# A four-layer graph network on one core: register range checks dropped, the edge network's sums moved to the front of VectorE's round, the first attention's one-hot moved to ScalarE

## The chip, the cores and the metric

The program runs on one core of a Trainium2 chip (trn2). The metric is the device time of one execution in microseconds (us); the number that counts is the median of several executions. A core has five engines that run side by side, each through its own instruction stream in order: TensorE (PE, with its weight loads listed as PEld), VectorE (DVE), ScalarE (ACT), GpSimd (POOL) and SyncE (SP). They wait for each other through semaphores. Each stream is driven by a sequencer (DVEq, ACTq, SPq in the rows), which also executes register arithmetic and which has to finish that before it can pass the next instruction to its engine.

## The reference

Four message-passing layers over 3125 nodes and 100000 edges, each on `h = relu(layernorm(x))`, each added to `x`. Edges are sorted by target `dst`. Cut to what matters:

```python
# layer 0, edge network (MLP)
h1  = relu([h[src], h[dst], edge_attr] @ We1 + be1)
em  = relu(h1 @ We2 + be2)
h2  = relu([h[dst], em] @ Wn1 + bn1)
x  += h + segment_sum(relu(h2 @ Wn2 + bn2), dst)
# layer 1, first attention: 4 heads, softmax over the edges of a target with its maximum taken off
e   = elu(s_src[src] + s_tgt[dst], 0.2);  ex = exp(e - segment_max(e, dst)[dst])
x  += segment_sum(ex / segment_sum(ex, dst)[dst] * xp[src], dst)
# layer 2, second attention: 8 heads, leaky relu, softmax without the maximum
# layer 3, relations: 16 weight matrices, chosen by the edge's type, summed by src
```

## The kernel before

The edges are cut into 208 blocks of 512 (`N_BLOCKS`, `BLOCK`); a block is two halves of 256 edges or four tiles of 128. All edges of a half have targets in one bin of 128 nodes. Four stages, one for each layer, run one after the other with a short node phase between them (normalisation, the node matrices and a table of rows in HBM). In each stage every block goes through the same steps:

- GpSimd fetches the source rows of a block from the table by four indirect DMAs, one for each tile (`gather`, L1032). ScalarE writes the indices that they use (`lay`, L1023); in the last stage VectorE does.
- VectorE compares the block's target numbers with 1..128. This gives the one-hot `hot` (edges by nodes), the left side of the matmul that sums a half's messages into its bin (`mm_sum`), and `hot_t`, the transposed one, which spreads target rows over edges.
- TensorE does the matmuls. `mm_sum` leaves two sums in a PSUM bank.
- VectorE adds the two sums to the accumulator `acc` at the bins of the halves (`add_sum`, L1335). Which bin that is stands in a table of numbers in SBUF, `bin_d`; `halves_of` (L997) loads eight of its numbers into registers at every fourth block. SyncE loads the halves' start addresses and, in the first attention, ScalarE loads bins, by the same helper.

`values_load_multi_w_load_instructions` with `min_val` and `max_val` emits one TENSOR_LOAD and, for each of the eight numbers, register arithmetic and an assertion that stops the program if the number is outside its range.

The order on each engine is written out by hand: `pipeline` and `unrolled` take a list of `(lag, stage)`. In round `k` an engine runs each stage of its list, in the list's order, for block `k - lag`. Nothing reorders it.

**Edge network (`edge_mlp`).** VectorE's round before is: `localize`, `make_hot_t`, `bring_dst` of block k, `nm_relu` of k-4, `make_hot` of k-2, `add_sum` of k-5, and then one small piece of a sort that the last layer needs. TensorE's round is `turn` (k-1), `mm_h2` (k-3), `mm_h1` (k-2), `mm_sum` (k-4), `mm_em` (k-2), `mm_nm` (k-3), `mm_q` (k-2). There is a single PSUM bank for the sums, so `mm_sum` of a block waits until `add_sum` of the block before has been done; it also waits for `nm_relu` of its own block.

**First attention (`softmax_sum`).** Groups of eight blocks share the steps that find the maxima: TensorE brings scores into lanes (`lanes`), ScalarE copies them out (`to_lanes`, L1575), VectorE scans (`tops`), TensorE turns back (`back`, L1632), VectorE subtracts (L1697), ScalarE takes the exponential (`weight`, L1581). In each block VectorE scales the rows (`message`, L1704) and makes `hot` (`make_hot`, L1709) from a copy of 1..128 in PSUM, TensorE sums (`mm_sum`, L1641), and ScalarE copies the sums out of one of two PSUM banks (`keep_sum`, L1590); `mm_sum` of block k waits for `keep_sum` of block k-2. The gather of a block waits for `mm_sum` of the block 16 before.

The two attentions' ScalarE streams and all streams of GpSimd and SyncE contain a hardware loop of 16 blocks a turn; VectorE's in the edge network and the second attention are written out in full.

## Time and profile before

| | us |
|---|---|
| median of three runs | 5009.35 (5000.32 to 5012.24) |
| the profiled execution's own time | 5033.62 |
| its span | 5031.8 |

Busy time over the span: PE 3496.0 (69%), PEld 2811.4 (56%), DVE 2828.2 (56%), ACT 1003.1 (20%), POOL 3291.4 (65%). No engine is busy all the time, and an average over the span says little, since the four stages have different limits. By stage the profile goes: ordering and first tables up to about 107 us; edge network up to 1343; node phase; first attention 1400 to 2665; node phase; second attention 2723 to 3805; node phase; relations 3945 to 5032.

In a timeline row the columns are start, duration, engine, line, operation with what it writes and reads, how many instructions are merged, and in brackets the idle time before it with what ended it. "issue" there means that the engine waited for nothing that the profile shows: often its own sequencer.

### The profile page before, as it was taken

The page shows a single profiled execution, that of the slowest core. Times are in us where ns is not written, and L with a number is a line of the kernel's source. Part 1 is how long each engine was busy: PE and PEld are TensorE (multiplying, and loading weights), DVE is VectorE, ACT ScalarE, POOL GpSimd, SP SyncE. Part 2 cuts the span into 40 slices and gives each one's busy share as a digit, 9 for nine tenths or more (in the row PEclk, how much of TensorE's full clock was granted, in tenths as well). Part 3 has the DMA queues.
Part 4 walks back from the last instruction along what each step waited for, and adds up shares of the span by engine and source line. Part 5 has one row for each costly group of instructions (what it writes and reads, how often), then busy time and mean ns, then how long its engine had stood idle before and what let it go on. Part 6 is the DMA issues. An engine that isn't in the chain of part 4 may idle for free. (4 is left out here: it accounts for less than half of the span.)

```text
span 5031.8 us, 89393 instructions
## 1 busy us (share of the span) xinstructions
PE 3496.0 (69%) x18874; PEld 2811.4 (56%) x18874; DVE 2828.2 (56%) x8555; ACT 1003.1 (20%) x3587; POOL 3291.4 (65%) x3348
## 2 busy tenths in 40 slices
PE   3989999999647777777763888778876543444433
PEld 2555555555447777777753778778773333333333
DVE  4566666655536666766776666666555433333332
ACT  3333333334211111111111222222221100000000
POOL 2766666666267767666732777777771477777776
PEclk7999999999755555555555555655567655555555
DMA  8445444444043333433411223332223422222222
GB/s 75 100 91 95 84 81 84 78 82 73 5 116 100 96 94 97 95 95 91 98 33 41 64 66 75 83 81 74 56 55 117 131 53 51 52 53 53 53 53 56
DMA packets 543241, 381.31 MB, mean 76 GB/s; under 512 B 360336, under 2 KB 495290, under 8 KB 539563
## 3 DMA queue, kind: packets, MB, share of 16 engines
q1 hardware_dynamic: 436392, 193.84, 17.3%
q0 software_dynamic: 106496, 184.24, 16.5%
q14 instruction: 312, 2.56, 0.2%
q8 instruction: 41, 0.67, 0.1%
HBM read 327.50 MB, written 35.53 MB: 72 GB/s over the span
## 5 line engine op out<-in xcount | busy, mean ns | idle before, releaser
L1032 POOL DMA_INDIRECT mlp_row<-tab,mlp_index x832 | 818.3, 984 | 476.6 <-ACT mlp_index L1023 248.4
L1032 POOL DMA_INDIRECT gat_row<-tab,gat_index x832 | 833.6, 1002 | 336.7 <-issue 231.0
L1032 POOL DMA_INDIRECT att_row<-tab,att_index x832 | 813.6, 978 | 253.6 <-issue 250.4
L1032 POOL DMA_INDIRECT rel_row<-tab,rel_index x832 | 803.8, 966 | 257.5 <-issue 227.5
L1424 PE MATMUL rel_ps_sum<-rel_row,rel_hot 128*128 128x128 f32 x1664 | 425.3, 437 | 648.1 <-DMA rel_row<-tab,rel_index 630.9
L1424 PEld LDWEIGHTS rel_ps_sum<-rel_row,rel_hot 128*128 128x128 f32 x1664 | 370.2, 327 | 703.7 <-DVE rel_hot L1449 384.8
L1641 PE MATMUL gat_ps_sum<-gat_row,gat_hot 128*128 128x136 f32 x1664 | 432.1, 438 | 241.3 <-DVE gat_hot L1709 153.8
L1843 PE MATMUL att_ps_sum<-att_row,att_hot 128*128 128x136 f32 x1664 | 420.8, 431 | 198.8 <-DVE acc L1335 194.9
L1641 PEld LDWEIGHTS gat_ps_sum<-gat_row,gat_hot 128*128 128x128 f32 x1664 | 374.2, 320 | 263.2 <-DVE gat_hot L1709 115.1
L1843 PEld LDWEIGHTS att_ps_sum<-att_row,att_hot 128*128 128x128 f32 x1664 | 374.9, 320 | 235.3 <-DVE acc L1335 230.1
L1335 DVE TENSOR_TENSOR acc<-acc,rel_ps_sum 128x128 f32 x416 | 119.6, 288 | 623.0 <-PE rel_ps_sum L1424 561.0
L1611 PEld LDWEIGHTS gat_ps_t<-gat_tgt,gat_hot_t 128*128 128x128 f32 x1664 | 366.4, 322 | 92.9 <-issue 47.3
L1611 PE MATMUL gat_ps_t<-gat_tgt,gat_hot_t 128*128 128x4 f32 x1664 | 347.1, 333 | 85.1 <-DVE gat_raw L1669 62.2
L1835 PEld LDWEIGHTS att_ps_t<-att_tgt,att_hot_t 128*128 128x128 f32 x1664 | 355.9, 312 | 0.6 <-ACT att_hot_t L1812 0.6
L1835 PE MATMUL att_ps_t<-att_tgt,att_hot_t 128*128 128x8 f32 x1664 | 331.0, 328 | 0.0
L1241 PE MATMUL mlp_ps_sum<-mlp_nm,mlp_hot 128*128 128x129 f32 x1664 | 242.8, 288 | 101.8 <-DVE acc L1335 101.6
L1241 PEld LDWEIGHTS mlp_ps_sum<-mlp_nm,mlp_hot 128*128 128x128 f32 x1664 | 203.0, 191 | 195.0 <-DVE acc L1335 139.0
L1298 DVE TENSOR_TENSOR mlp_nm<-mlp_ps_nm,mlp_less 128x512 f32<-128x512 f32 x208 | 143.4, 689 | 196.5 <-PE mlp_ps_nm L1232 186.2
L1826 PE MATMUL att_ps_hot<-ident,att_hot 128*128 128x128 f32 x832 | 208.2, 399 | 33.1 <-DVE att_hot L1856 33.1
L1156 ACT ACTIVATE mlp_em<-mlp_ps_em,be 128x512 f32<-128x512 f32 x208 | 142.9, 687 | 388.6 <-PE mlp_ps_em L1214 374.4
L1335 DVE TENSOR_TENSOR acc<-acc,att_ps_sum 128x136 f32 x416 | 122.1, 293 | 145.2 <-issue 111.9
L1335 DVE TENSOR_TENSOR acc<-acc,mlp_ps_sum 128x129 f32 x416 | 119.7, 288 | 137.0 <-issue 104.6
(284 smaller groups left out, 5906.0 us busy)
## 6 DMA issues: line engine op xcount, KB each, us to landing
mlp_aim<-in_dst SPq DMA_DIRECT2D x416, 128.0 KB
gat_aim<-in_dst SPq DMA_DIRECT2D x416, 128.0 KB
mlp_row<-in_edge_attr SPq DMA_DIRECT2D x416, 64.0 KB
tab<-n_stage SPq DMA_DIRECT2D x25, 1024.0 KB
mlp_row<-tab,mlp_index POOLq DMA_INDIRECT x832
gat_row<-tab,gat_index POOLq DMA_INDIRECT x832
att_row<-tab,att_index POOLq DMA_INDIRECT x832
rel_row<-tab,rel_index POOLq DMA_INDIRECT x832
```

The source lines that it names most:

```text
L1032: gp.indirect_dma_start(rows[n][b][:, t, :], None, tables[n], bass.IndirectOffsetOnAxis(index[b][:, n, t:t + 1], axis=0)).then_inc(s_g[b], 16)
L1156: act.activation(em[b % 2][:].rearrange("p (h f) -> p h f", h=2), p_em, ACT.Relu, bias=g.be2[:]).then_inc(s_emr, 1)
L1241: mm = pe.matmul(half_sum(p_sum, t // HALF_TILES, D + 1), hot[b % RING][:, t, :], nm[b % 2][:, t, :], start=(t % HALF_TILES == 0), stop=(t ...
L1298: v.tensor_tensor(nm[b % 2][:, :, 0:D].rearrange("p (h t) f -> p h t f", h=2), p_nm.rearrange("p h (t f) -> p h t f", f=D), less[:].unsque ...
L1335: v.tensor_tensor(there, there, half_sum(bank, h, width).unsqueeze(1), ALU.add).then_inc(s_acc, 1)
L1424: mm = pe.matmul(half_sum(p_sum[b % 2], t // HALF_TILES, D), hot[b][:, t, :], row[b][:, t, :], start=(t % HALF_TILES == 0), stop=(t % HALF ...
L1611: mm = pe.matmul(p_t[:, at:at + H], hot_t[b % RING][:, t * P:(t + 1) * P], tgt[b][:, t // HALF_TILES, :], start=True, stop=True)
L1641: mm = pe.matmul(half_sum(p_sum[b % 2], t // HALF_TILES, ROW), hot[b % 4][:, t, :], rows[:, b, t, :], start=(t % HALF_TILES == 0), stop=(t ...
L1826: mm = pe.transpose(p_hot[b % 2][:, t * P:(t + 1) * P], hot[b][:, t, :], g.ident[:])
L1835: mm = pe.matmul(p_t[b % 2][:, t * T:(t + 1) * T], hot_t[b % 2][:, t * P:(t + 1) * P], tgt[b][:, t // HALF_TILES, :], start=True, stop=True)
L1843: mm = pe.matmul(half_sum(p_sum[b % 2], t // HALF_TILES, W), hot[b][:, t, :], flat[b][:, t, :], start=(t % HALF_TILES == 0), stop=(t % HAL ...
```

## The change

Three edits:

1. `halves_of` passes a reason to skip the range check, so a TENSOR_LOAD is all that is left of a fetch of eight numbers. It serves all engines and stages. The numbers are clipped where the tables are made.
2. In the edge network VectorE's round begins with `add_sum` of block k-5 and `nm_relu` of k-4; the other stages follow in their old order, and the piece of the sort stays last.
3. In the first attention `make_hot` moves from VectorE to ScalarE. It takes two steps there: `measure_gap` writes (target - number)² for each tile (four ACTIVATE Square, the target a bias column, lag 14), and `make_hot` writes relu(1 - that) for the whole block (one ACTIVATE Relu, lag 15), which is 1 where they are equal and 0 elsewhere, since both are whole numbers. Both stand ahead of `keep_sum` in ScalarE's list. The copy of 1..128 in PSUM goes, and `s_init` counts to 3 in place of 4.

```diff
-            values[:] = nc.values_load_multi_w_load_instructions(where, [engine], min_val=0, max_val=most)[1]
+            values[:] = nc.values_load_multi_w_load_instructions(
+                where, [engine], min_val=0, max_val=most,
+                skip_runtime_bounds_check_because="the table is clipped to this range where it is made")[1]
...
-            unrolled([(0, localize), (0, make_hot_t), (0, bring_dst), (4, nm_relu), (2, make_hot),
-                      (5, add_sum(nc, v, g, g.bin_d, p_sum, D + 1, 1, s_sum, s_acc, s_tick))],
+            unrolled([(5, add_sum(nc, v, g, g.bin_d, p_sum, D + 1, 1, s_sum, s_acc, s_tick)), (4, nm_relu),
+                      (0, localize), (0, make_hot_t), (0, bring_dst), (2, make_hot)],
...
+        gap = [c.sb(f"gap{b}", [P, TILES, P]) for b in range(2)]
...
+            def measure_gap(k, q, b):
+                ge(act, s_hot, k - 1)
+                tick(act, s_tick)
+                for t in range(TILES):
+                    ins = act.activation(gap[b % 2][:, t, :], g.iota[:], ACT.Square, scale=-1.0,
+                                         bias=g.rec_d[:, bass.ds(k * TILES + t, 1), 1].bitcast(F32))
+                ins.then_inc(s_gap, 1)
+
+            def make_hot(k, q, b):
+                act.wait_ge(s_gap, k + 1)
+                ge(act, s_sum, k - 3)
+                act.activation(hot[b % 4][:], gap[b % 2][:], ACT.Relu, scale=-1.0, bias=1.0).then_inc(s_hot, 1)
...
-                           (6, at_end(to_lanes)), (9, at_end(weight)), (19, keep_sum), (21, at_end(fade_exp))], WIDE)
+                           (6, at_end(to_lanes)), (9, at_end(weight)), (14, measure_gap), (15, make_hot), (19, keep_sum), (21, at_end(fade_exp))], WIDE)
...
-            def make_hot(k, q, b):
-                ge(v, s_sum, k - 3)
-                v.tensor_tensor(hot[b % 4][:], iota.unsqueeze(1).broadcast_to([P, TILES, P]), rec_f(g.rec_d, k),
-                                ALU.is_equal).then_inc(s_hot, 1)
...
-                         (8, at_end(subtract)), (16, message), (16, make_hot), (19, at_end(fades)),
+                         (8, at_end(subtract)), (16, message), (19, at_end(fades)),
```

VectorE in the edge network, around a round whose `add_sum` fetches bins. Before, from `nm_relu` to the next round's start (ISA stands for register instructions, `mlp_ps_nm` is what `mm_nm` wrote, `mlp_own` the first step of `localize`):

```order
L1298 TENSOR_TENSOR mlp_nm1<-mlp_ps_nm,mlp_less 128x4x128
L1282 TENSOR_TENSOR mlp_hot3<-iota,rec_d 128x512
L1005 TENSOR_LOAD bin_d
L1005 ISA x16
L1335 ISA
L1335 TENSOR_TENSOR acc<-acc,mlp_ps_sum 128x129
L1335 ISA
L1335 TENSOR_TENSOR acc<-acc,mlp_ps_sum 128x129
L1266 TENSOR_TENSOR mlp_own0<-rec_d,first 128x4
```

After, the beginning of such a round:

```order
L1005 TENSOR_LOAD bin_d
L1337 ISA
L1337 TENSOR_TENSOR acc<-acc,mlp_ps_sum 128x129
L1337 ISA
L1337 TENSOR_TENSOR acc<-acc,mlp_ps_sum 128x129
L1300 TENSOR_TENSOR mlp_nm1<-mlp_ps_nm,mlp_less 128x4x128
L1268 TENSOR_TENSOR mlp_own1<-rec_d,first 128x4
```

The sixteen register instructions between the load and the sums are gone, and the sums stand ahead of `nm_relu` in place of behind `nm_relu` and `make_hot`.

ScalarE in the first attention, the round in which `weight` closes a group and bins are fetched. Before:

```order
L1023 COPY gat_index0<-rec_d 128x4
L1005 TENSOR_LOAD bin_d
L1005 ISA x16
L1556 ISA
L1556 COPY gat_tgt0<-tgt 128x4
L1556 ISA
L1556 COPY gat_tgt0<-tgt 128x4
L1581 ACTIVATE gat_ps_wgt<-gat_less 128x128
L1582 ACTIVATE gat_row<-gat_ps_back 128x4x8x4
L1590 COPY gat_sums<-gat_ps_sum1 128x272
```

After:

```order
L1025 COPY gat_index0<-rec_d 128x4
L1005 TENSOR_LOAD bin_d
L1558 ISA
L1558 COPY gat_tgt0<-tgt 128x4
L1558 ISA
L1558 COPY gat_tgt0<-tgt 128x4
L1583 ACTIVATE gat_ps_wgt<-gat_less 128x128
L1584 ACTIVATE gat_row<-gat_ps_back 128x4x8x4
L1592 ACTIVATE gat_gap0<-iota,rec_d 128x128 x4
L1599 ACTIVATE gat_hot1<-gat_gap1 128x512
L1605 COPY gat_sums<-gat_ps_sum1 128x272
```

Between `weight` and the copy of the sums (`keep_sum`) there are now five more ACTIVATEs; in a round without `weight` or `to_lanes` they stand in the same place, right ahead of `keep_sum`. The list of ScalarE's instructions holds no more table loads than before.

## Rows read from the trace of the kernel before

**Rows 1.** Busy time by stage: stretch, length, each engine's busy time, clock, DMA share, GB/s.
```profile
143.00:1343.00 1200.00, 1097.36 (x8216) 628.52 (x8212) 733.89 (x2423) 453.02 (x1219) 789.90 (x806) 0.96 0.43 80
1400.00:2665.00 1265.00, 917.49 (x4160) 873.55 (x4160) 828.56 (x2114) 201.45 (x1015) 836.50 (x833) 0.53 0.37 90
```

**Rows 2.** Groups of instructions, POOL, whole run: busy, mean ns, idle before by releaser.
```profile
L1032 POOL DMA_INDIRECT gat_row<-tab,gat_index x832 | 833.6, 1002 | 336.7 <-issue 231.0 <-ACT gat_index L1023 84.8 <-PE gat_ps_sum L1641 21.0
L1032 POOL DMA_INDIRECT mlp_row<-tab,mlp_index x832 | 818.3, 984 | 476.6 <-ACT mlp_index L1023 248.4 <-issue 228.2
L1032 POOL DMA_INDIRECT att_row<-tab,att_index x832 | 813.6, 978 | 253.6 <-issue 250.4 <-ACT att_index L1023 1.7 <-PE att_ps_sum L1843 1.5
L1032 POOL DMA_INDIRECT rel_row<-tab,rel_index x832 | 803.8, 966 | 257.5 <-issue 227.5 <-DVE rel_index L1437 30.0
```

**Rows 3.** Waits of POOL, relations: total, times, longest.
```profile
POOL rel_row L1032 <- DVE rel_index L1437: 30.0, 86, 4.1
```

**Rows 4.** Line L1032: count, ns min/median/max, first and last start.
```profile
L1032 POOL DMA_INDIRECT mlp_row<-tab,mlp_index x832: 942/947/3097, 106.7 to 1309.6; - x167
L1032 POOL DMA_INDIRECT gat_row<-tab,gat_index x832: 942/947/3057, 1404.6 to 2572.9; - x167
```

**Rows 5.** Waits of PE, edge network: total, times, longest.
```profile
PE mlp_ps_sum L1241 <- DVE acc L1335: 101.6, 95, 2.1
```

**Rows 6.** Timeline of PE, edge network: four `mm_sum`, 700 to 724 us.
```profile
702.19 1.16 PE L1241 MATMUL mlp_ps_sum<-mlp_nm,mlp_hot 128*128 128x129 f32 x8 [0.52 <-DVE acc L1335]
...
708.70 1.16 PE L1241 MATMUL mlp_ps_sum<-mlp_nm,mlp_hot 128*128 128x129 f32 x8 [1.35 <-DVE acc L1335]
...
713.80 1.16 PE L1241 MATMUL mlp_ps_sum<-mlp_nm,mlp_hot 128*128 128x129 f32 x8
...
718.89 1.16 PE L1241 MATMUL mlp_ps_sum<-mlp_nm,mlp_hot 128*128 128x129 f32 x8
```

**Rows 7.** Timeline of DVE around the second of them.
```profile
704.67 0.69 DVE L1298 TENSOR_TENSOR mlp_nm<-mlp_ps_nm,mlp_less 128x512 f32<-128x512 f32 x1 [0.44 <-issue]
705.28 0.68 DVE L1282 TENSOR_TENSOR mlp_hot<-iota,rec_d 128x512 f32<-128x512 f32 x1
707.92 0.73 DVE L1335 TENSOR_TENSOR acc<-acc,mlp_ps_sum 128x129 f32 x2 [1.96 <-issue]
```

**Rows 8.** Line L1005, the fetch of table numbers, sequencers: ns min/median/max.
```profile
L1005 DVEq FUSED_REGOPS  x2133: 57/183/196, 107.8 to 4996.3; - x194
L1005 DVEq SEQ_ASSERT  x2080: 23/23/33, 108.1 to 4996.6; - x190
...
L1005 DVEq TENSOR_LOAD <-bin_d x208: 590/597/825, 107.2 to 3795.6; - x104
```

**Rows 9.** Busy time of one group of eight blocks, first attention.
```profile
1903.70:1950.74 47.04, 36.47 (x160) 34.80 (x161) 31.84 (x82) 7.75 (x41) 32.70 (x34) 0.50 0.41 94
```

**Rows 10.** Timeline of PE in that group: its waits over 1.5 us.
```profile
1903.70 2.15 PE L1641 MATMUL gat_ps_sum<-gat_row,gat_hot 128*128 128x136 f32 x8 [1.65 <-ACT gat_sums L1590]
...
1909.01 2.18 PE L1641 MATMUL gat_ps_sum<-gat_row,gat_hot 128*128 128x136 f32 x8 [1.67 <-DVE gat_hot L1709]
...
1921.54 2.18 PE L1641 MATMUL gat_ps_sum<-gat_row,gat_hot 128*128 128x136 f32 x8 [1.78 <-ACT gat_sums L1590]
...
1928.47 2.15 PE L1641 MATMUL gat_ps_sum<-gat_row,gat_hot 128*128 128x136 f32 x8 [3.25 <-DVE gat_hot L1709]
```

**Rows 11.** Timeline of ACT in that group: `weight` and the copy behind it.
```profile
1920.74 0.28 ACT L1581 ACTIVATE gat_ps_wgt<-gat_less 128x128 f32<-128x128 f32 x1 [11.14 <-DVE gat_row L1704]
1921.11 0.38 ACT L1590 COPY gat_sums<-gat_ps_sum 128x272 f32<-128x272 f32 x1
```

**Rows 12.** Groups of instructions: the one-hot, and ACT shapes near the new ones.
```profile
L1709 DVE TENSOR_TENSOR gat_hot<-gat_ps_iota,rec_d 128x512 f32<-128x512 f32 x208 | 141.6, 681 | 0.0
L635 ACT ACTIVATE TMP<-X,mu 128x128 f32<-128x128 f32 x25 | 9.7, 388 | 0.2
L1156 ACT ACTIVATE mlp_em<-mlp_ps_em,be 128x512 f32<-128x512 f32 x208 | 142.9, 687 | 388.6 <-PE mlp_ps_em L1214 374.4 <-issue 14.2
```

More of the change, by code:

```diff
@@ L1482, in softmax_sum @@
         fifth = c.sb("fifth", [P, 1])
-        p_t, p_iota, p_wgt = c.ps("t"), c.ps("iota"), c.ps("wgt")
+        p_t, p_wgt = c.ps("t"), c.ps("wgt")
         wgt = p_wgt[:, 0:TILES * LANES].rearrange("p (t i h) -> p t i h", t=TILES, h=H)
-        iota = p_iota[:, 0:P]
         p_sum = [c.ps(f"sum{b}") for b in range(2)]
@@ L1489, in softmax_sum @@
         (s_ix, s_init, s_hot_t, s_tgt, s_t, s_low, s_fifth, s_e, s_loc, s_lane, s_laned, s_run, s_top, s_back, s_less,
-         s_wgt, s_msg, s_hot, s_sum, s_kept, s_most, s_arg, s_fade, s_part, s_scaled, s_mul, s_acc) = (
+         s_wgt, s_msg, s_hot, s_sum, s_kept, s_most, s_arg, s_fade, s_part, s_scaled, s_mul, s_acc, s_gap) = (
             c.sem(n) for n in ("ix init hot_t tgt t low fifth e loc lane laned run top back less wgt msg hot sum kept "
-                               "most arg fade part scaled mul acc").split())
+                               "most arg fade part scaled mul acc gap").split())
         block = c.block()
@@ L1547, in _ @@
             lay = gather_stages(act, None, *io, WIDE)[0]
-            act.wait_ge(s_init, 4)
+            act.wait_ge(s_init, 3)
             bins = halves_of(nc, ACTE, g.bin_d, N_BINS - 1)
@@ L1596, in _ @@
             pipeline(act, [(0, lay), (0, bring_tgt), (4, at_end(bring_local)), (5, at_end(fifth_exp)),
-                           (6, at_end(to_lanes)), (9, at_end(weight)), (19, keep_sum), (21, at_end(fade_exp))], WIDE)
+                           (6, at_end(to_lanes)), (9, at_end(weight)), (14, measure_gap), (15, make_hot), (19, keep_sum), (21, at_end(fade_exp))], WIDE)
         @block.tensor
         def _(pe):
-            pe.wait_ge(s_init, 4)
+            pe.wait_ge(s_init, 3)
             def take(k, q, b):
@@ L1653, in _ @@
             v.memset(fifth[:], math.log(0.2)).then_inc(s_init, 1)
-            v.tensor_copy(iota, g.iota[:]).then_inc(s_init, 1)
-            v.wait_ge(s_init, 4)
+            v.wait_ge(s_init, 3)
             def make_hot_t(k, q, b):
```

## The prediction, made blind

> **What bounds the kernel now.** I read the busy time by stage first, then the fetching engine's groups of instructions, then TensorE's waits, and last the timelines at the places where it waits. The stages don't overlap, so each has its own limit.
>
> GpSimd's indirect DMAs set a floor for every stage. Busy time and its own "issue" gaps make 818.3 + 228.2 = 1046 us in the edge network, 833.6 + 231.0 = 1065 in the first attention, 813.6 + 250.4 = 1064 in the second, 803.8 + 227.5 = 1031 in the relations [rows 2]. What lies above that floor is what GpSimd waited for others: 248 us in the edge network, 84.8 + 21.0 = 106 in the first attention, 3 in the second. The 30 of the relations are 86 waits with 4.1 us in the longest [rows 3], 0.3 us each for the rest, the gap that every one of these DMAs has ahead of it anyway (228 us over 832). So only the first two stages have anything to give, 354 us together, and none of the edits touches the DMAs themselves.
>
> Edge network: TensorE is busy 1097 of 1200 us at a granted clock of 0.96 [rows 1], and its only wait as a group is for VectorE's sums, 101.6 us in 95 waits [rows 5]. The timeline shows the shape: from one `mm_sum` to the next 6.51 us where the bins were fetched just ahead of the sums, 5.10 and 5.09 where nothing was waited for [rows 6]. In that one round VectorE finished `make_hot` at 705.96 and began the sums at 707.92, with 1.96 us of "issue" [rows 7]; those are the fetch. TensorE without waits needs 208 x 5.09 = 1059 us, just above GpSimd's 1046. The stretch from the first gather to the last is 1203 us now [rows 4].
>
> First attention: here TensorE runs at the lower of its two clocks (0.53 granted over the stage, 0.50 in the group shown) and is busy 36.47 us of a group's 47.04 [rows 1, 9]. It waits 10.57 us: 1.67 and 3.25 for `make_hot` on VectorE, 1.65 and 1.78 for `keep_sum` on ScalarE [rows 10], and the rest, 2.2 us, in pieces under 1.5 us. ScalarE is late with `keep_sum` because it stands in order behind `weight` (11.14 us of waiting) and `to_lanes`; once it is released, the copy follows 0.37 us later [rows 11].
>
> **The change part by part.**
>
> *Range checks.* For each number the sequencer does 183 ns of register work and a 23 ns assertion on VectorE [rows 8]. Eight make 1.65 us, and the gaps that the timeline shows are 1.96 us with part of the load's 0.60 us hidden. What is left of a fetch is the load. VectorE assertions: 2080, so 260 fetches, 104 of them in the edge network and 52 in each other stage. That frees at least 104 x 1.65 = 172 us of VectorE in the edge network and 86 in the first attention. Of this only what TensorE or GpSimd waits for counts. In the two last stages GpSimd's floor hides it: nothing there, or at most the 3 us of waits. On ScalarE and SyncE the same eight checks go, by VectorE's rows at most 1.7 us a fetch, which shortens the way to the first gather of a stage. I take 4 us for all stage starts together (bounds 0 and 8: four starts, at most 2 us of a checked fetch in each).
>
> *Sums first in the edge network.* `mm_sum` of k-5 is ready two matmul groups before `mm_nm` of k-4 is, so the sums (0.73 us) fit in VectorE's wait for `mm_nm` in place of following two 0.69 us instructions. `nm_relu` began at 704.67 [rows 7], so `mm_nm` was done by then, and TensorE came to its next `mm_sum` at 708.70 - 1.35 = 707.35 [rows 6], 2.7 us later; of VectorE only the sums and `nm_relu`, 1.4 us, must fit ahead of that. What now comes behind (`localize`, `make_hot_t`, `bring_dst`, `make_hot`) is used two TensorE rounds later and has room: VectorE's busy time is 734 us over 208 blocks [rows 1], 3.5 us a block, with two plain loads for each four blocks 3.8 us, against a round of 5.09. Either edit alone would remove most of the 1.35 us wait; together they leave nothing of it that I can find. So TensorE loses its 101.6 us. At most the stage falls to 208 x 5.09, which is 144 us less; the difference of 42 us is mostly short spells at the lower clock (0.96 granted), some of which follow the waits. I take 114: the waits, and 12 of the 42. Bounds: 60, if GpSimd's rate of 5.03 us a block, almost TensorE's, shows through as new waits, and 144. What is late next is TensorE itself, then GpSimd.
>
> *The one-hot on ScalarE.* VectorE loses 208 instructions of 0.68 us, about 0.61 us each from start to start (a row of 705.28 after one of 704.67 [rows 7]): 4.9 us a group. With two checks a group (3.3 us or more) VectorE's work falls from 31.8 to about 27 us busy, so it no longer paces TensorE, and the 1.67 + 3.25 + 2.2 = 7.1 us of waits for it go.
>
> ScalarE gains four 128x128 instructions with a bias column, and one of 128x512. The trace has both shapes: 388 ns and 687 ns [rows 12]. Instructions in a row overlap (0.28 us long, next one later by less [rows 11]), so I take 0.30 us for each of the four and 0.60 for the last, 1.8 us a block; bounds 1.4 and 2.2 (4 x 0.388 + 0.687 without overlap). By the Trainium skill's "ScalarE: Activation LUTs", section "What ACT_TABLE_LOAD costs", an ACTIVATE with a [128,1] pointer bias takes about 280 ns plus 0.833 ns an element, 387 ns here, which the row's 388 bears out; with its overlap of 93 ns and an immediate bias in the last one the five would be an estimated 1.7 us, and the sum would come out 5 us lower.
>
> ScalarE's own load stays small: 201 us busy [rows 1] plus 208 x 1.8 = 374 is under half of the stage. But the five stand ahead of `keep_sum`, and twice a group TensorE waits for a `keep_sum` that is behind a released `to_lanes` or `weight`. Each of these two waits grows by 1.8 us. The group then takes 36.47 + 3.43 + 2 x 1.8 = 43.5 us, 3.5 less than 47.04; GpSimd's floor is 1065 / 26 = 40.9. 26 groups give 92 us. Behind the last gather, where the stage still runs 2665 - 2574 = 91 us [rows 4] and VectorE paces, about 11 one-hots and a few checks go, some 10 us; I take off about as much for new small waits in the coupling, and say 90 for the stage. Bounds: -30 (each wait grows by a second ScalarE round of 2.8 us and VectorE's gain only just covers it) and 116 (GpSimd's waits all gone, and the 10).
>
> *Sum.* 114 + 90 + 4 = 208 us off the profiled execution's 5033.6, 4826. The median of the runs shown is 24 us below that execution; the same 208 off 5009.35 give 4801, and I say 4800.
>
> **The rivals.**
>
> *Only the edge network gains.* ScalarE's five instructions ahead of `keep_sum` eat what VectorE gives: TensorE's waits for `gat_sums`, 3.43 us a group, become 10 or more. For it: two waits a group already end at ScalarE. Against it: ScalarE is busy 7.75 us of the group's 47 [rows 9], so 14 more leave it idle more than half of the time. 5009 - 118, with up to 20 us from the tail: 4875 to 4895.
>
> *Both stages fall to GpSimd's floor.* If TensorE waited so little in the first attention that its granted clock rose to the upper level, the group's 36 us would shrink well below 40.9, and 116 us come off; in the edge network 144, at starts 4. 5009 - 264 = 4745. The rows speak against it more than for it: 78% busy at 0.50 [rows 9] beside 91% busy at 0.96 [rows 1], so busy time alone doesn't bring the clock there. The Trainium skill's "TensorE: Matmul & The Clock Gate", section "What's actually happening", says that sustained activity releases the throttle; that speaks for this rival, and the group shown agrees only in part.
>
> *ScalarE becomes the chain of the first attention, and the kernel is slower.* The one-hots are then late too: after each of the two long waits TensorE needs ScalarE to catch up three blocks, 3 x 2.8 = 8.4 us in place of the 1.8 above. The group takes 43.5 + 2 x 6.6 = 56.7 us, 9.7 more than before, 251 over 26 groups: 5009 - 118 + 251 = 5142. It decides from a group of 47.04 + 118/26 = 51.6 us on; two blocks of catching up (51.1 us) would leave no change. Against it: ScalarE's list lets it be several blocks ahead of TensorE between the long waits, and `make_hot` of k stands four rounds ahead of the `keep_sum` of k.
>
> *The change doesn't do what it says* hardly applies: the order shows the checks and the old one-hot gone and no new table load in ScalarE's stream.
>
> **How the numbers follow.** Forecast, 0.63, with its own range 4750 to 4870 (gains of 85 to 144 in the edge network, 50 to 110 in the first attention). Only the edge network, 0.17. GpSimd's floor, 0.12. ScalarE's chain, 0.08: slower in 0.05, about even in 0.03. The range that leaves out 2 in 10 is 4750 to 4900: it takes in the first rival, and the upper part of the second. A measurement of this kernel tells about 0.3%, 15 us, from no change. Faster by more than that: 0.92; within it 0.03; slower 0.05.
>
> **What would show it.** Right: in the edge network TensorE's wait for `acc` falls from 101.6 us to under 20, and `mm_sum` follows `mm_sum` by 5.1 us in every round; the stage's gathers span about 1090 us. No SEQ_ASSERT is left on line 1005. In the first attention the waits for the one-hot vanish from the list, those for `gat_sums` grow from 3.4 to some 7 us a group, a group takes 43 to 44 us, and the clock stays near 0.5. The second attention and the relations keep their length within 5 us. Wrong: TensorE waits in the edge network for gathered rows or for `nm_relu`; a group of the first attention at 47 us or more; a wait for ScalarE's `hot` over 2 us; a clock well over 0.6 in that stage.

## The result, and the profile after

The changed kernel takes 4846.53 us (median of four, 4836.64 to 4850.77), the kernel before on the same chip 5004.84 (4998.07 to 5012.24): ratio 0.9679 [0.9664, 0.9694], 158 us less. The forecast of 4800 was 46 us too low. The profiled execution took 4850.8 us with a span of 4849.0, against 5033.6 and 5031.8.

From the first and the last start of the gathers of each stage (they add up to the spans' difference of 183 us):

| us | before | after | |
|---|---|---|---|
| edge network, first to last gather | 1202.9 | 1091.9 | -111.0 |
| from there to the first attention's first gather | 95.0 | 79.6 | -15.4 |
| first attention, first to last gather | 1168.3 | 1140.5 | -27.8 |
| from there to the second attention's first gather | 153.7 | 134.1 | -19.6 |
| second attention, first to last gather | 1066.1 | 1054.3 | -11.8 |
| node phase, and the relations' gathers | 159.5 + 1056.3 | 154.6 + 1063.7 | +2.5 |

Of the 15.4 us, 14.7 are the end of the edge network itself: TensorE started its last `mm_sum` there 32.3 us behind the start of the last gather before (1341.9 and 1309.6) and 17.6 us after (1216.5 and 1198.9).

**GpSimd.** Groups of instructions of the kernel after, whole run, columns as in [rows 2]:

```profile
L1034 POOL DMA_INDIRECT gat_row<-tab,gat_index x832 | 849.2, 1021 | 293.4 <-issue 224.7 <-PE gat_ps_sum L1656 46.8 <-ACT gat_index L1025 21.8
L1034 POOL DMA_INDIRECT mlp_row<-tab,mlp_index x832 | 839.6, 1009 | 344.7 <-issue 241.4 <-ACT mlp_index L1025 103.0 <-PE mlp_ps_row L1178 0.3
L1034 POOL DMA_INDIRECT rel_row<-tab,rel_index x832 | 811.3, 975 | 255.5 <-issue 234.1 <-DVE rel_index L1439 21.4
L1034 POOL DMA_INDIRECT att_row<-tab,att_index x832 | 802.0, 964 | 253.4 <-issue 250.4 <-PE att_ps_sum L1852 2.4 <-ACT att_index L1025 0.6
```

GpSimd's waits in the edge network fell from 248 us [rows 2] to 103, nearly all of it ahead of the first blocks. But the same 832 gathers are busy for 839.6 us instead of 818.3, 1009 ns each instead of 984. Nothing in the change touches them.

**TensorE in the edge network.** Waits, and its timeline where [rows 6] stood:

```profile
PE mlp_ps_row L1178 <- DMA mlp_row<-tab,mlp_index: 46.4, 34, 20.8
...
PE mlp_ps_sum L1243 <- DVE mlp_nm L1300: 0.2, 1, 0.2
```

```profile
703.29 1.16 PE L1243 MATMUL mlp_ps_sum<-mlp_nm,mlp_hot 128*128 128x129 f32 x8
708.39 1.16 PE L1243 MATMUL mlp_ps_sum<-mlp_nm,mlp_hot 128*128 128x129 f32 x8
714.12 1.16 PE L1243 MATMUL mlp_ps_sum<-mlp_nm,mlp_hot 128*128 128x129 f32 x8
719.64 1.16 PE L1243 MATMUL mlp_ps_sum<-mlp_nm,mlp_hot 128*128 128x129 f32 x8
```

The 101.6 us for `acc` [rows 5] are gone. What is new are waits for gathered rows: 34, of which one, at the stage's start, is 20.8 us. One round here takes 5.10, two others 5.73 and 5.52. In those rounds TensorE has caught up with GpSimd, and GpSimd sets the pace.

**First attention.** Waits from 1280 to 2600 us (total, times, longest), then the `weight` place of [rows 11] on ScalarE:

```profile
PE gat_ps_sum L1656 <- ACT gat_sums L1605: 132.6, 41, 3.7
...
PEld gat_ps_sum L1656 <- ACT gat_hot L1599: 123.1, 33, 3.8
...
PE gat_ps_sum L1656 <- DVE gat_row L1718: 46.9, 15, 3.7
```

```profile
1830.26 0.28 ACT L1583 ACTIVATE gat_ps_wgt<-gat_less 128x128 f32<-128x128 f32 x1 [10.27 <-DVE gat_row L1718]
1830.47 0.26 ACT L1584 ACTIVATE gat_row<-gat_ps_back 128x128 f32<-128x128 f32 x1
1830.63 1.26 ACT L1592 ACTIVATE gat_gap<-iota,rec_d 128x128 f32<-128x128 f32 x4
1831.80 0.61 ACT L1599 ACTIVATE gat_hot<-gat_gap 128x512 f32<-128x512 f32 x1
1832.32 0.36 ACT L1605 COPY gat_sums<-gat_ps_sum 128x272 f32<-128x272 f32 x1
```

The five new instructions take 1.69 us from first start to the copy (1830.63 to 1832.32), where 1.8 was taken; the copy that followed `weight` 0.37 us later [rows 11] now follows it after 2.06. TensorE waits over 3.6 us here:

```profile
1832.24 0.69 DVE L1718 TENSOR_TENSOR gat_row<-gat_row,gat_ps_wgt 128x528 f32<-128x528 f32 x1
...
1832.89 1.86 PEld L1656 LDWEIGHTS gat_ps_sum<-gat_row,gat_hot 128*128 128x128 f32 x8 [3.75 <-ACT gat_hot L1599]
1832.92 2.15 PE L1656 MATMUL gat_ps_sum<-gat_row,gat_hot 128*128 128x136 f32 x8 [3.64 <-DVE gat_row L1718]
```

The last two rows are one and the same pause, once for the weight load (whose weights are the one-hot) and once for the matmul. The one-hot ended at 1832.41, the copy at 1832.68 and VectorE's `message` at 1832.93, so `message` came last. It is like that for all 33 waits of the weight loads for `gat_hot`: each lies in a pause of the matmuls that ended later, 23 times with the copy and 10 times with `message`. The 123.1 us must therefore not be added to the others. No matmul waits for ScalarE's one-hot as the last to come.

Both stages where they now lie, and one group of the first attention, columns as in [rows 1, 9]:

```profile
107.00:1218.00 1111.00, 1069.56 (x8320) 618.86 (x8320) 750.15 (x2469) 460.75 (x1246) 839.59 (x832) 1.00 0.48 89
1274.00:2491.00 1217.00, 927.72 (x4160) 890.88 (x4160) 708.25 (x1905) 533.03 (x2055) 852.10 (x833) 0.52 0.37 93
```

```profile
1799.69:1843.09 43.40, 35.48 (x161) 34.13 (x161) 26.99 (x75) 20.46 (x79) 33.05 (x32) 0.54 0.42 102
```

TensorE's clock in the edge network went from 0.96 to 1.00 as its waits went; in the first attention it stayed at the lower level (0.52). The group shown takes 43.40 us.

### The profile page after: what moved, and what is told of

It is laid out like the page before. It is cut to its first block and busy times, and to the rows that moved or that the text cites. A ratio compares the mean times of both kernels' runs of the same rounds, so it can differ in the third digit from the quotient of the medians.

```text
span 4849.0 us, 82599 instructions
## 1 busy us (share of the span) xinstructions
PE 3518.8 (73%) x18874; PEld 2832.8 (58%) x18874; DVE 2704.2 (56%) x8346; ACT 1324.1 (27%) x4627; POOL 3324.2 (69%) x3348
## 5 line engine op out<-in xcount | busy, mean ns | idle before, releaser
L1034 POOL DMA_INDIRECT mlp_row<-tab,mlp_index x832 | 839.6, 1009 | 344.7 <-issue 241.4
L1034 POOL DMA_INDIRECT gat_row<-tab,gat_index x832 | 849.2, 1021 | 293.4 <-issue 224.7
L1852 PE MATMUL att_ps_sum<-att_row,att_hot 128*128 128x136 f32 x1664 | 442.3, 445 | 126.3 <-DVE acc L1337 122.7
L1656 PEld LDWEIGHTS gat_ps_sum<-gat_row,gat_hot 128*128 128x128 f32 x1664 | 389.0, 331 | 194.6 <-ACT gat_hot L1599 123.1
L1626 PEld LDWEIGHTS gat_ps_t<-gat_tgt,gat_hot_t 128*128 128x128 f32 x1664 | 380.2, 333 | 105.9 <-issue 63.0
L1626 PE MATMUL gat_ps_t<-gat_tgt,gat_hot_t 128*128 128x4 f32 x1664 | 359.0, 340 | 98.2 <-DVE gat_raw L1683 78.3
L1844 PEld LDWEIGHTS att_ps_t<-att_tgt,att_hot_t 128*128 128x128 f32 x1664 | 368.2, 322 | 0.2 <-ACT att_hot_t L1821 0.2
L1592 ACT ACTIVATE gat_gap<-iota,rec_d 128x128 f32<-128x128 f32 x832 | 264.8, 391 | 0.0
L1826 ACT ACTIVATE att_ps_wgt<-att_val 128x32 f32<-128x32 f32 x208 | 41.8, 201 | 770.3 <-DVE att_row L1882 770.3
L1874 DVE TENSOR_TENSOR att_val<-att_row,att_ps_t 128x32 f32<-128x32 f32 x208 | 42.8, 206 | 326.2 <-DMA att_row<-tab,att_index 326.2
## 6 DMA issues: line engine op xcount, KB each, us to landing
mlp_aim<-in_dst SPq DMA_DIRECT2D x416, 128.0 KB
gat_aim<-in_dst SPq DMA_DIRECT2D x416, 128.0 KB
```

Of the source, the lines that this page charges most:

```text
L1034: gp.indirect_dma_start(rows[n][b][:, t, :], None, tables[n], bass.IndirectOffsetOnAxis(index[b][:, n, t:t + 1], axis=0)).then_inc(s_g[b], 16)
L1592: ins = act.activation(gap[b % 2][:, t, :], g.iota[:], ACT.Square, scale=-1.0, bias=g.rec_d[:, bass.ds(k * TILES + t, 1), 1].bitcast(F32))
L1626: mm = pe.matmul(p_t[:, at:at + H], hot_t[b % RING][:, t * P:(t + 1) * P], tgt[b][:, t // HALF_TILES, :], start=True, stop=True)
L1656: mm = pe.matmul(half_sum(p_sum[b % 2], t // HALF_TILES, ROW), hot[b % 4][:, t, :], rows[:, b, t, :], start=(t % HALF_TILES == 0), stop=(t ...
L1826: act.activation(wgt, val[b][:], ACT.Exp).then_inc(s_wgt, 1)
L1844: mm = pe.matmul(p_t[b % 2][:, t * T:(t + 1) * T], hot_t[b % 2][:, t * P:(t + 1) * P], tgt[b][:, t // HALF_TILES, :], start=True, stop=True)
```

## The experiments

Each edit was first made alone. "Gathers" is always first to last start of a stage's gathers in one profiled execution; ratios are against the kernel before on the same chip.

**Only the range checks dropped.**

```diff
-                where, [engine], min_val=0, max_val=most)[1]
+                where, [engine], min_val=0, max_val=most,
+                skip_runtime_bounds_check_because="...")[1]
```

> The kernel before with only the range checks dropped. Theory A (each edit takes its part: in the edge network either of the first two frees TensorE, in the first attention the shorter VectorE round and the move of the one-hot share the gain): edge network gathers 1203 us down to about 1095, TensorE's wait for the sums from 102 us to under 20; first attention about 25 to 35 us shorter; total 4860 to 4885. Rival B (the checks do it all and the one-hot's move brings nothing or costs): total 4835 to 4850, as fast as the changed kernel.

Measured 4814.62 us, ratio 0.9565 [0.9547, 0.9583]: one edit brings more than all three, and more than either expectation allowed. Edge network's gathers 1061.6 us, first attention's 1109.4. Its two groups on GpSimd:

```profile
L1034 POOL DMA_INDIRECT gat_row<-tab,gat_index x832 | 844.0, 1014 | 267.4 <-issue 233.5 <-ACT gat_index L1025 19.3 <-PE gat_ps_sum L1643 14.7
L1034 POOL DMA_INDIRECT mlp_row<-tab,mlp_index x832 | 809.1, 973 | 344.4 <-issue 250.7 <-ACT mlp_index L1025 93.8
```

The gathers of the edge network are back at 973 ns. So the changed kernel's 1009 come from another edit.

**Only the order.**

```diff
-            unrolled([(0, localize), (0, make_hot_t), (0, bring_dst), (4, nm_relu), (2, make_hot), (5, add_sum(...))],
+            unrolled([(5, add_sum(...)), (4, nm_relu), (0, localize), (0, make_hot_t), (0, bring_dst), (2, make_hot)],
```

> The kernel before with only the sums moved to the front of VectorE's round in the edge network. Theory A: TensorE's wait for the sums falls from 102 us to under 25, edge network gathers about 1100 us, the other stages unchanged; total 4895 to 4915. Rival (the checks' register work, now ahead of the sums and of nm_relu, still delays both): wait of 40 us or more left and total 4935 or more.

Measured 4998.08, ratio 0.9932 [0.9912, 0.9953]. The theory missed by some 90 us; what was given as the rival came out. TensorE's longest group of waits in the edge network:

```profile
PE mlp_ps_sum L1241 <- DVE mlp_nm L1298: 82.6, 52, 3.3
```

The check work still stands ahead of the sums, and `nm_relu` behind them is late instead of `acc`: 82.6 us for 101.6. The order mostly passes the wait on; the stage's gathers span 1170.9 us instead of 1202.9.

**Only the one-hot on ScalarE.**

> The kernel before with only the first attention's one-hot on ScalarE. Theory A: first attention 15 to 35 us shorter, other stages unchanged; total 4970 to 4990. Rival B: no change or slower, 5000 to 5030, with TensorE's waits for gat_sums at least doubled from 87 us.

Measured 4999.04, ratio 0.9944 [0.9927, 0.9961]. First attention's gathers 1152.1 instead of 1168.3, as in theory A, while TensorE's wait for `gat_sums` (1280 to 2600 us) is 128.0 us, not doubled as the rival had it; the edge network still waits 101.2 us for `acc`.

**Checks and order, without the one-hot; checks and one-hot, without the order.**

> The changed kernel with the first attention's one-hot left on VectorE. Theory A: edge network as in the changed kernel (gathers 1092 us), first attention 20 to 30 us longer than there; total 4865 to 4875. Rival B: 4847 or less.

> The changed kernel with the edge network's order as before: checks dropped and one-hot on ScalarE. If the edits add up, edge network as with the checks alone (gathers 1062 us), first attention as in the changed kernel (gathers 1140, 20 us less behind them): total 4815 to 4825. If the one-hot's move costs on top of dropped checks: 4830 or more, above the checks alone (0.9565 of the kernel before). If it gains: under 4800.

Measured 4857.79, 0.9654 [0.9633, 0.9675], and 4819.36, 0.9624 [0.9600, 0.9648]. In the first of them theory A fails: the first attention's gathers take 1128.3 us, 12 less than in the changed kernel and not 20 to 30 more. The second lies in the range given for edits that add up, yet its ratio is above that of the checks alone. Laid side by side: alone, order and one-hot bring 0.7% and 0.6%. Behind the dropped checks they cost 0.9% and 0.6%, and both together 1.2% (each ratio is good to 0.2%). In the edge network the split is clean: gathers of 1089.9 us with the new order, 1060.6 without it, whatever the rest.

**`keep_sum` ahead of the two new ScalarE steps.** The changed kernel, with one place moved:

```diff
-  (9, at_end(weight)), (14, measure_gap), (15, make_hot), (19, keep_sum), (21, at_end(fade_exp))], WIDE)
+  (9, at_end(weight)), (19, keep_sum), (14, measure_gap), (15, make_hot), (21, at_end(fade_exp))], WIDE)
```

> The changed kernel with keep_sum ahead of measure_gap and make_hot in ScalarE's list, nothing else. Theory A (the five ACTIVATEs ahead of keep_sum hold up mm_sum after each long ScalarE wait): TensorE's wait for gat_sums falls from 133 us to 60 or less, a group from 44.2 to about 42, the first attention 30 to 50 us shorter, total 4800 to 4820 where the changed kernel has 4847. Rival: the one-hot is then what TensorE waits for, and the stage stays within 10 us.

Measured 4804.23, ratio 0.9592 [0.9571, 0.9614]. First attention's gathers 1102.6 instead of 1140.5. Waits from 1280 to 2600 us:

```profile
PE gat_ps_sum L1656 <- ACT gat_sums L1605: 88.7, 51, 2.0
...
PE gat_ps_sum L1656 <- DVE gat_row L1718: 55.0, 38, 4.6
...
PEld gat_ps_sum L1656 <- ACT gat_hot L1599: 30.3, 22, 2.3
```

The wait for the copy is back to what it was (87.3 us in 50 before), though not at the 60 or less of the expectation. The weight loads' waits for the one-hot fall from 123 to 30, though in the round it is now made later; all 22 again lie in matmul pauses that end with `message`.

The lengths of a group (first and last start of the subtraction, 25 groups apart), before, after and here:

```profile
L1697 DVE TENSOR_TENSOR gat_less<-gat_score,gat_ps_back x26: 286/288/289, 1464.3 to 2602.7; 128x128 f32<-128x128 f32 x26
```

```profile
L1711 DVE TENSOR_TENSOR gat_less<-gat_score,gat_ps_back x26: 286/288/289, 1338.1 to 2443.0; 128x128 f32<-128x128 f32 x26
```

```profile
L1711 DVE TENSOR_TENSOR gat_less<-gat_score,gat_ps_back x26: 286/288/289, 1335.3 to 2405.1; 128x128 f32<-128x128 f32 x26
```

That is 45.54, 44.20 and 42.79 us a group. TensorE's time between these two starts (for the checks alone 1309.8 to 2388.1), in us over 25 groups, with its matmul waits by what came last:

| | before | checks alone | after | copy first |
|---|---|---|---|---|
| length | 1138.4 | 1078.3 | 1104.9 | 1069.8 |
| busy | 870.1 | 875.9 | 881.6 | 869.7 |
| `mm_sum` for the one-hot | 143.7 | 66.7 | 0 | 0 |
| `mm_sum` for `message` | 0 | 0 | 43.5 | 48.9 |
| `mm_sum` for the copy | 85.5 | 85.3 | 127.7 | 86.9 |
| `gat_ps_t` for VectorE's scores of fetched rows | 38.1 | 50.5 | 52.0 | 64.2 |

Moving the copy to the front takes 40.8 us off the wait for the copy; some of it comes back in the last row. VectorE's scores in turn wait for fetched rows: 44.2 us before, 129.8 after, 116.3 with the copy first.

**What lengthens the gathers: two ways to take the new order's pair apart.** In the new order `make_hot` (128x512, both inputs in SBUF) stands directly ahead of the sort's piece (the same). First the one-hot by four `tensor_scalar` with one tile input each, then `make_hot` moved up behind `nm_relu`:

```diff
-                v.tensor_tensor(hot[b % RING][:], g.iota[:].unsqueeze(1).broadcast_to([P, TILES, P]), rec_f(g.rec_d, k), ALU.is_equal)
+                for t in range(TILES):
+                    ins = v.tensor_scalar(hot[b % RING][:, t, :], g.iota[:], g.rec_d[:, bass.ds(k * TILES + t, 1), 1].bitcast(F32), None, ALU.is_equal)
```

```diff
-  (4, nm_relu), (0, localize), (0, make_hot_t), (0, bring_dst), (2, make_hot)],
+  (4, nm_relu), (2, make_hot), (0, localize), (0, make_hot_t), (0, bring_dst)],
```

> The changed kernel with the edge network's one-hot made by four tensor_scalar instructions (one input from SBUF and a column) in place of one tensor_tensor with two inputs from SBUF. Theory C (a VectorE instruction with two SBUF inputs holds up GpSimd's indirect DMA, and the new order puts make_hot and the sort's piece, both such, back to back): the DMAs of 1.3 us and more go from 64 to under 15, GpSimd's busy time in the edge network from 840 to about 810 us, its gathers from 1092 to about 1065 us, total 4820. Rival D (the lengthening has to do with the DMAs' data, not with VectorE): no change in either, 4847 or a little more for the longer VectorE round.

> The changed kernel with make_hot moved from the end of VectorE's edge network round to the place right behind nm_relu, so that it no longer touches the sort's piece. Theory C: the DMAs of 1.3 us and more go from 64 to about 15, gathers to about 1065 to 1075 us, total 4820 to 4830. Rival (any order with the sums first costs GpSimd the same): gathers 1090 us, total 4847.

Measured 4812.48 and 4815.10, both 0.9616 [0.9594, 0.9638]; the edge network's gathers 1062.2 and 1065.2 us at 973 and 977 ns. Both bring the 30 us back. The next pair was to confirm the pair theory from the other side, by adding load in the old order: a second one-hot into a tile that nothing reads, as one instruction with two SBUF inputs, or as four with one tile input.

```diff
+                ge(v, s_spare, k)
+                v.tensor_tensor(spare[:], g.iota[:].unsqueeze(1).broadcast_to([P, TILES, P]), rec_f(g.rec_d, k), ALU.is_equal).then_inc(s_spare, 1)
                 v.tensor_tensor(hot[b % RING][:], ...)
```

> Checks dropped, one-hot on ScalarE, old order in the edge network, and a second one-hot of the same shape (128x512, both inputs in SBUF, about 0.68 us) made into a spare tile directly ahead of make_hot, 208 times: nothing reads it. VectorE has the room (804 of 1200 us busy without it). If it is a stretch of back-to-back instructions with two SBUF inputs that holds up GpSimd's gather instruction, then this one gives what the changed kernel's order gave: mean of a gather instruction in the edge network about 1005 to 1015 ns instead of 971, some 50 to 80 of them over 1.25 us instead of 2, and gathers spread over 1085 to 1100 us instead of 1061. Rival (it is something else in the order, such as the wait for the accumulation or the timing of the tick instructions): mean within 10 ns of 971 and gathers over 1061 +/- 5 us.

> As the kernel with the extra one-hot of two SBUF inputs, but the extra one is made by four tensor_scalar instructions with one tile input each (about 0.28 us each, 1.1 us together, so VectorE is busy for longer than with the extra two-source one). If two SBUF inputs are what counts: mean 971 +/- 10 ns, fewer than 15 gather instructions over 1.25 us, gathers over 1061 to 1068 us. Rival (any busy VectorE at that place slows GpSimd): mean over 1000 ns and gathers at 1085 us or more.

Both came out the other way round. With the extra two-input instruction: mean 974 ns, one gather over 1.25 us, gathers over 1062.4 us, 4836.15 us in all (0.9628). With the four one-input ones: mean 1018 ns, 1098.9 us, 4866.83 us in all (0.9689). Neither "back to back" nor "the number of inputs of what is added" is the cause, and the pair theory falls. The timelines point to what is. VectorE and GpSimd in the kernel with the four extra ones:

```profile
706.77 0.89 DVE L1287 TENSOR_SCALAR mlp_spare<-iota,rec_d 128x128 f32<-128x128 f32 x4
707.58 0.67 DVE L1290 TENSOR_TENSOR mlp_hot<-iota,rec_d 128x512 f32<-128x512 f32 x1
708.18 0.71 DVE L1343 TENSOR_TENSOR acc<-acc,mlp_ps_sum 128x129 f32 x2
```

```profile
706.60 0.94 POOL L1034 DMA_INDIRECT mlp_row<-tab,mlp_index  x1 [0.30 <-ACT mlp_index L1025]
707.85 1.22 POOL L1034 DMA_INDIRECT mlp_row<-tab,mlp_index  x1 [0.30 <-issue]
709.37 0.94 POOL L1034 DMA_INDIRECT mlp_row<-tab,mlp_index  x1 [0.30 <-issue]
```

and in the one with the extra two-input instruction:

```profile
708.07 0.68 DVE L1286 TENSOR_TENSOR mlp_spare<-iota,rec_d 128x512 f32<-128x512 f32 x1
708.67 0.68 DVE L1288 TENSOR_TENSOR mlp_hot<-iota,rec_d 128x512 f32<-128x512 f32 x1
```

```profile
708.62 0.95 POOL L1034 DMA_INDIRECT mlp_row<-tab,mlp_index  x1 [0.30 <-issue]
```

The gather of 707.85 starts inside `make_hot`, whose successor starts at 708.18, 0.33 us later, and it is 0.28 us longer than the 0.94 usual. The gather of 708.62 starts 0.05 us before a `make_hot` begins, lies beside the whole of it, and is not lengthened; nor is that `make_hot`. In the changed kernel the gather starts 0.04 us into one:

```profile
707.83 0.68 DVE L1284 TENSOR_TENSOR mlp_hot<-iota,rec_d 128x512 f32<-128x512 f32 x1
708.43 0.68 DVE L397 TENSOR_TENSOR words<-words_in 128x512 f32<-128x512 f32 x1
```

```profile
707.87 1.47 POOL L1034 DMA_INDIRECT mlp_row<-tab,mlp_index  x1 [0.30 <-issue]
```

and is 0.53 us longer, again about the rest of the one instruction and not of both. Counted over each trace: in the changed kernel 83 gathers of the edge network begin 0.02 to 0.35 us into a `make_hot` or a sort's piece. Taking 0.12 us off the listed remainder (the last part says why), 407 ns of it are left on average, and the gathers are 393 ns longer, 33 us together; in the kernel with four extra instructions 158, 298 and 289 ns; in the old order with the checks dropped one or two begin so early, and the others meet only its end. And where an input lies in PSUM the effect is absent. In the kernel before, first attention, the one-hot reads 1..128 from PSUM:

```profile
1537.16 0.68 DVE L1709 TENSOR_TENSOR gat_hot<-gat_ps_iota,rec_d 128x512 f32<-128x512 f32 x1
```

```profile
1537.23 0.95 POOL L1032 DMA_INDIRECT gat_row<-tab,gat_index  x1 [0.30 <-issue]
```

35 gathers begin so early within that instruction, with 406 ns left on average by the same count, and none is over 12 ns longer. So by these counts it is the instant at which a gather starts. Order and extra instructions matter through the phase between GpSimd's four gathers a block and VectorE's round. Why each kernel settles at the phase it has was not tried.

**The parts that pay, together, beside the checks alone once more.** The best of each: checks dropped, old order, one-hot on ScalarE with the copy first.

> The range checks dropped, the one-hot of the first attention on ScalarE, VectorE's round of the edge network in its old order, and ScalarE's copy keep_sum ahead of measure_gap and make_hot. If the two gains that the runs so far showed are apart from each other (the edge network's gathers at 1061 us in the old order, the first attention's at 1103 us with the copy first), the time is the changed kernel's 4846.5 less 31 and less 38: 4778 us, span of mlp gathers 1061 +/- 3, of gat gathers 1103 +/- 5. Rival: they share a cause (an earlier start or another phase of the sort in the edge network), and then one of the two stage times is not reproduced and the total stays above 4800.

> The range checks dropped and nothing else, a second time, so that it stands on the same chip as the best combination. Theory: 0.9565 of before again, within 0.002, and slower than the combination by about 25 to 30 us (gat gathers 1109 against 1103, and the tail behind them and the last stages some 15 us shorter where ScalarE makes the one-hot). Rival: the 0.9565 was that chip's, and the ratio comes out at 0.962 or above.

On one chip 4794.20 (4792.92 to 4795.51), ratio 0.9545 [0.9526, 0.9564], and 4803.95 (4802.64 to 4811.91), 0.9563 [0.9544, 0.9583]. The combination is the fastest kernel run here. Both stage times came out as expected (gathers 1060.7 and 1105.1 us), so the two gains are apart from each other. The total is 16 us above the expectation. Against the changed kernel's trace 69 us were expected and 56 came: 4.2 went back in the second attention's gathers and 2.5 in the relations', whose code is the same, 3.9 between edge network and first attention, 2.6 in the latter. The first kernel's 0.9565 is reproduced. But it is only 10 us behind the combination, not 25 to 30, and the ratios' intervals overlap: that moving the one-hot is worth anything once the checks are gone rests on a difference of 0.2% and on the runs not overlapping.

## Why the prediction was right or wrong

**Right in sign and in the place of the limits, 46 us too low.** The forecast was 114 + 90 + 4 = 208 off the profiled execution's time; it was 183 there and 158 by medians. Before's profiled execution stood 29 us over its median in these runs, after's 4; the rest is the terms. By the table of gathers: 111.0 for 114 in the edge network, 27.8 + 19.6 = 47.4 for 90 in the first attention, 15.4 between the two, where only the 4 of all stage starts stood, and 11.8 - 2.5 = 9.3 for 0 in the last two stages. That the total came as near as 25 us is partly luck: the first attention brought half of its term, and gains that had no term made up for part of it.

*Edge network, 114: measured 111, and that it agrees is luck: 141 from one edit, less 30 lost by another.* The wait for `acc` went, as said. Dropping the checks alone took 141 us (1202.9 to 1061.6), the top of the bounds given (144): TensorE at clock 1.00 and, behind the stage's start, almost without waits, at 208 x 5.10. It needs no other edit. The step that failed is "what now comes behind ... has room". VectorE has; what was not looked at is which of GpSimd's instructions it meets. The moved `make_hot` and the sort's piece cost (1009 - 973) x 832 = 30 us on the engine that had been named as only 1% behind TensorE. The list of what would show it wrong held that "TensorE waits in the edge network for gathered rows", and this did come. "Either edit alone would remove most of the 1.35 us wait" failed for the order: 82.6 us came back as waits for `nm_relu`. And the sum counted only up to the last gather; TensorE's lag behind it shrank by another 14.7 us.

*First attention, 90: measured 28 between the gathers and 20 behind the last.* The tail was to give some 10, and gave 20, of which 12 are there with the checks alone (141.9 us for 153.7). In the stage itself the saving is a difference of waits, since the group's 36.47 us of busy time stand on both sides of it: 7.1 us of waits were to go and 3.6 to come, 3.5 less. The table of the 25 groups has, per group, 10.7 us of waits before (10.57 in the one group read) and 8.9 after: 1.8 less, and 0.5 more of busy time, so 1.34 in all. That the group forecast at 43.5 came out at 43.4 where I looked is chance; the mean is 44.2. "Each of these two waits grows by 1.8" was right for the long ones: the longest went from 2.0 to 3.7. But there are 41 of them for 50, and all together grew by 1.7 a group, not 3.6. The step that failed is the other one, that the 7.1 us of waits for VectorE would simply go. The matmuls no longer wait for the one-hot (5.7 a group before), but for `message` they now wait 1.7, and the waits for the scores, which with small ones for the one-hot made up the 2.2, rose from 1.5 to 2.1: 3.4 went in place of 7.1. The wait for ScalarE's one-hot of over 2 us, named as a sign of failure, does stand in the rows of the weight loads (up to 3.8), but there as a part of the pauses for the copy and for `message`. It is ScalarE all the same that holds up the copy: moving the copy in front takes 38 us off the gathers, so the cause was in the order of ScalarE's list, not in its load of 20.5 us a group. The lower bound of -30 does not follow from its own terms: two waits longer by 4.6 each against 7.1 saved would be 2.1 a group more, some 55 us, or 45 with the tail's 10. No run came near it. And [rows 11] leave out the instruction of 1920.95 between the two shown, 0.21 us behind the first; it is the overlap on which the 0.30 rested, and the five measured 1.69 us where 1.8 was taken.

The granted clock stayed at the lower level, 0.52 over the stage (0.53 before [rows 1]) and 0.54 in the group, with TensorE 82% busy in it, so the case of GpSimd's floor in both stages fell. The Trainium skill's "TensorE: Matmul & The Clock Gate", section "What's actually happening", says that sustained activity releases the throttle; in this stage the throttle stayed.

*Stage starts, 4, and the last two stages, 0.* The edge network's first gather starts where it did (107.0 for 106.7). The second attention's gathers are 11.8 us shorter, forecast as at most 3, and the relations' 7.4 longer, forecast to stay within 5. In the second attention the kernels without checks lie between 1051.2 and 1063.3, those with them between 1064.3 and 1066.4, so a few us may be the checks; the rest is not explained by any run here.

What stays open: in the kernel with checks and order the first attention's gathers take 1128.3 us and in that with the checks alone 1109.4 and 1113.6, with identical code from there on. Some 15 us hang on something that no run here isolates.

## What to carry to other kernels

Take a part of a change off again before crediting it: here one of three edits brought more than the three together, and the other two, as they were placed, each looked useful only while it was missing. Add up a stage's waits over all its groups, by what came last for the matmul; a weight load's wait beside a matmul's can be the same pause twice. And when a step is moved on VectorE in a stage that GpSimd's gathers pace, look at what reads two SBUF operands at the moments at which the gathers start; and on an engine that runs a list in order, put what another engine waits for ahead of what is needed later.

## What the runs showed of the hardware

**A gather that starts inside a VectorE instruction with both inputs in SBUF is lengthened by what is left of it.** With the instruction taken to end 0.08 us before its listed end (the cadence of 0.60 for a listed 0.68) and the gather to need it 0.04 us after its start, the lengthening met the remainder within 17 ns for 511 of the 513 gathers that began 0.02 to 0.35 us into such an instruction (`make_hot`, its extra copy, the sort's pieces) in the edge network, over fourteen traces. In the first attention it is up to 2.1 us, where the gather meets the 2.35 us product over `gat_sums`. The `tensor_scalar` of `hot_t`, with one tile input in SBUF, does the same by up to about 0.15 us. Instructions with one input in PSUM don't: in the changed kernel's trace over 100 gathers began inside `nm_relu` and none was over 10 ns longer, and over 110 inside `message`, longer by 0 ns in the mean.

The two exceptions began 0.02 and 0.03 us into the instruction. There the gather keeps its length and VectorE's instruction is longer, 0.75 us for 0.68 in the kernel with only the one-hot on ScalarE:

```profile
856.89 0.75 DVE L1282 TENSOR_TENSOR mlp_hot<-iota,rec_d 128x512 f32<-128x512 f32 x1
856.92 0.94 POOL L1032 DMA_INDIRECT mlp_row<-tab,mlp_index  x1 [1.67 <-ACT mlp_index L1023]
```

A `make_hot` that starts in the same instant as a gather takes 0.72 us (at 1074.80 in the kernel before), one that starts 0.05 us after it its usual 0.68. So both can be held up, but not alike: the gather delays VectorE by at most about 0.07 us in these rows, and VectorE the gather by all that is left of its instruction.

The Trainium skill's "SBUF — State Buffer", section "Who interferes with whom", says that an instruction of VectorE with two SBUF inputs contends with a GpSimd instruction that reads SBUF, and one with at most one outside the two-port modes does not. The rows with two SBUF inputs and those with one in PSUM agree; whether `hot_t` runs in a two-port mode no run here shows. Of VectorE's two-port modes the same section says that "Whoever issues first gets the shared pair for the whole instruction". With two SBUF inputs it is also the first who goes ahead here, but a gather's turn, under 0.07 us, is far shorter than its 0.94 us. This reading was made from the traces behind the last runs; no kernel was made to shift the phase alone.

**Range checks on register loads are dear.** Eight checked numbers held up VectorE for about 1.7 us (8 x (183 + 23) ns of its sequencer [rows 8]), and leaving out 260 such fetches on VectorE and those on two other engines was worth 4.4% of this kernel.

**Five ScalarE instructions in a row** (four of 128x128 with a bias column, one of 128x512) follow each other faster than their lengths add up, 1.69 us for 4 x 0.39 + 0.61 = 2.17.
